# One block of a perceiver: every second query feature unit takes its minimum on GpSimd and its relu on VectorE instead of ScalarE

## The reference

```
x = x + cross_attention(layernorm(x), ctx)       # 16 heads, softmax over 512 context rows
x = x + linear_attention(layernorm(x))           # below
x = x + experts(layernorm(x))                    # 16 experts, top 8 tokens each, and a shared MLP of 1024

# linear attention, 16 heads of 32, 128 features
elu1(y) = where(y > 0, y + 1, exp(y))
q_proj = elu1(q @ proj);  k_proj = elu1(k @ proj)
kv  = sum over tokens of k_proj (x) v ;  k_sum = sum over tokens of k_proj
out = (q_proj @ kv) / (q_proj @ k_sum + 1e-8) @ w_out + b_out
```

## Time and profile before

| | |
|---|---|
| median of 3 executions | 666.02 us (664.43 to 666.73) |
| the profiled execution | 663.74 us, span 661.9 us |
| PE, DVE, ACT, POOL busy over the span | 96%, 47%, 39%, 5% |
| feature units of queries: exp, relu on ACT | 0.60, 0.59 us each, 16 of each |
| their joining instruction on DVE | 0.69 us each, 16 |
| granted TensorE clock | full in all stretches |

### The profile page before, as it was taken

One profiled execution on the slowest core, in us unless ns is written; L12 is line 12 of the kernel. 1 busy time (PEld: TensorE's weight loads), 2 busy tenths in 40 slices (PEclk: granted clock), 3 DMA queues, 4 the chain that ended last, 5 costly groups with the idle time before them and its releaser, 6 DMA issues.

```text
span 661.9 us, 10401 instructions
## 1 busy us (share of the span) xinstructions
PE 636.7 (96%) x4216; PEld 413.3 (62%) x4216; DVE 312.5 (47%) x643; ACT 255.4 (39%) x488; POOL 34.8 (5%) x38
## 2 busy tenths in 40 slices
PE   6989999999999999999998998999999999999997
PEld 5758777777778787678887664444444444343433
DVE  4965636354454516655778785423223222323123
ACT  5645536354545535546776252111121212211110
POOL 0300000000000000636000000000000000000000
PEclk9999999999999999999999999999999999999999
DMA  8211010101150000030319644989999999999972
GB/s 297 101 63 65 2 64 1 65 11 54 71 249 0 2 1 1 2 112 0 132 36 429 248 179 179 374 357 399 394 417 414 406 400 402 393 377 388 375 295 72
DMA packets 14347, 129.55 MB, mean 196 GB/s; under 512 B 2720, under 2 KB 2848, under 8 KB 6240
## 3 DMA queue, kind: packets, MB, share of 16 engines
q1 hardware_dynamic: 12576, 127.15, 49.1%
q10 hardware_dynamic: 1728, 1.77, 0.8%
HBM read 125.90 MB, written 1.05 MB: 192 GB/s over the span
## 4 chain that ended last, share of the span: by engine, by line
PE 78%; DVE 8%; DMA 5%; ACT 5%; ACTq 2%; issue 2%; SPq 1%; DVEq 0%
PE ps L1214 23%; PE ps L1501 14%; PE ps L1538 7%; PE ps L1511 5%; PE ps L1408 5%; DMA w_u<-in_wu 4%; PE ps L1284 4%; PE ps L1357 3%; PE ps L1551 3%; PE ps L1260 3%; PE ps L1295 2%; PE ps L1325 2%; PE ps L1455 2%; ACTq L396 2%; PE ps L1467 1%
## 5 line engine op out<-in xcount | busy, mean ns | idle before, releaser
L1538 PE MATMUL ps<-w_d,hid_T 128*64 128x512 f32 x256 | 58.2, 596 | 1.0 <-issue 0.7
L1501 PE MATMUL ps<-w_u,x_slot 128*64 128x512 f32 x256 | 58.1, 595 | 1.0 <-DMA w_u<-in_wu 1.0
L1501 PE MATMUL ps<-w_g,x_slot 128*64 128x512 f32 x256 | 58.1, 595 | 0.8 <-ACT x_slot L779 0.8
L582 ACT ACTIVATE probs<-ps,neg_max 128x512 f32<-128x512 f32 x64 | 43.5, 687 | 39.1 <-DVE neg_max L898 39.1
L741 ACT ACTIVATE hid<-ps 128x512 f32<-128x512 f32 x24 | 14.4, 598 | 102.6 <-PE ps L1501 76.8
L1214 PE MATMUL ps<-wv_hi,ctx_hi 128*128 128x512 f32 x128 | 51.6, 403 | 0.5 <-ACT v_s L563 0.5
L878 DVE COPY probs_T<-ps 128x512 f32<-128x512 f32 x28 | 19.4, 692 | 64.8 <-PE ps L1284 64.8
L1214 PE MATMUL ps<-wv_lo,ctx_hi 128*128 128x512 f32 x128 | 49.9, 390 | 0.0
L1214 PE MATMUL ps<-wv_hi,ctx_lo 128*128 128x512 f32 x128 | 49.9, 390 | 0.0
L898 DVE TENSOR_REDUCE neg_max<-ps 128x1 f32<-128x512 f32 x64 | 39.7, 682 | 18.4 <-PE ps L1260 18.3
L1076 DVE TENSOR_TENSOR hid<-hid,ps 128x512 f32<-128x512 f32 x24 | 16.5, 687 | 65.2 <-PE ps L1501 35.6
(11 more groups left out here) (246 smaller groups left out, 1183.0 us busy)
## 6 DMA issues: line engine op xcount, KB each, us to landing
w_u<-in_wu SPq DMA_DIRECT2D x16, 2048.0 KB, 15.7
w_d<-in_wd SPq DMA_DIRECT2D x16, 2048.0 KB, 12.0
w_g<-in_wg SPq DMA_DIRECT2D x16, 2048.0 KB, 13.2
ctx_raw<-in_ctx SPq DMA_DIRECT2D x7, 1024.0 KB, 4.8
w_qkv<-in_wqkv SPq DMA_DIRECT2D x1, 3072.0 KB, 15.2
ws_g<-in_wsg SPq DMA_DIRECT2D x1, 2048.0 KB, 7.8
ws_u<-in_wsu SPq DMA_DIRECT2D x1, 2048.0 KB, 7.9
ws_d<-in_wsd SPq DMA_DIRECT2D x1, 2048.0 KB, 21.3
```

The lines of the kernel that those rows point to most:

```text
L582: act.activation(probs[:, p, :], bank(SCORE[p]), ACT.Exp, bias=neg_max[:, p:p + 1], scale=1.0, accum_out=row_sum[:, p:p + 1]).then_inc(exp ...
L1501: ins = pe.matmul(ps[64 * fh:64 * (fh + 1), dst, :], x_slot[:, e, dt, :], weights[e % 2][:, dt, BANK * fh:BANK * (fh + 1)], start=(dt == 0 ...
L1538: ins = pe.matmul(ps[64 * fh:64 * (fh + 1), 6 + side(n), :], hid_T[:, side(n), j, 64 * fh:64 * (fh + 1)], w_d[e % 2][:, KT * fh + j, :], s ...
```

## The change

For odd units from 16 on (17, 19, ... 31: eight units) ACT does the exponential only. GpSimd takes the minimum with one, in place in `exps`, when `fexp_done` says that the exponential is there, and signals `fmin_done`. DVE waits for that and computes max(PSUM, 0) + exps in one instruction, which reads one operand from PSUM and one from SBUF. The even query units and all key units stay as they are. In GpSimd's stream the eight minima stand between the row bias and the wait for the output projection.

```diff
+        fmin_done = sem("fmin_done")
...
         def act_relus(u):
 
-            return u % 2 == 0 or u >= NT * KT
+            return u % 2 == 0
+
+        def pool_mins(u):
+
+            return not act_relus(u) and u >= NT * KT
...
             add_row_bias(1, bout_rows)
+            for u in range(2 * NT * KT):
+                if pool_mins(u):
+                    pool.wait_ge(fexp_done, u + 1)
+                    pool.tensor_scalar(exps[:, u % 3, :], exps[:, u % 3, :], 1.0, None, ALU.min).then_inc(fmin_done, 1)
             pool.wait_ge(res_ps, 2 * NT)
...
                                                  op1=ALU.add).then_inc(feat_done, 1)
+                    elif pool_mins(u):
+                        dve.wait_ge(fmin_done, sum(pool_mins(v) for v in range(u + 1)))
+                        dve.scalar_tensor_tensor(out=dst, in0=bank(u % 3), scalar=0.0, in1=exps[:, u % 3, :],
+                                                 op0=ALU.max, op1=ALU.add).then_inc(feat_done, 1)
```

## The result

The changed kernel took 669.98 us (median of 10 runs, 667.81 to 674.69) beside 664.75 us for the kernel before (10 runs on the same chip): a ratio of 1.0081, with an interval of 1.0062 to 1.0101. It is slower by 5.2 us, which is outside the 0.3% within which nothing could be told. One of the ten executions of before took 813.78 us, the other nine 663.21 to 666.73; without it their median is 664.43 and the loss 5.5 us, and the ratio compares undisturbed executions only. "The same" had been the likeliest, at 667.4 us; the median lies 0.02 us inside the upper end of the range. The profiled execution took 670.76 us, its span 668.7; that of before took 663.74 and 661.9.

A forecast was written before the change was run, and what follows sets the result against it. The prediction took TensorE, busy 96%, as the bound, with query units short through turn-taking waits. Delays of +0.6 at att(0,0), +1.0 by unit 27 and +1.3 by unit 31 became +1.4 on 666.02: 667.4 us, range 665.0 to 670.0.

The forecast's parts named there:

- "The same": Whole kernel: a time within about 0.3%, 2.0 us either way, of the kernel before; chance 0.61.
- What bounds the kernel: TensorE, busy 96% of the span; the change acts from 338.8 to 361.4 us, where TensorE idles 2.8 us.
- the number to watch: Start of att(1,0) on TensorE, 361.36 us before; forecast at 362.7 to 362.8.
- The break-even: Odd query units, exp to join: the new way takes 0.71 us plus the minimum, so it pays only under 0.49.
- the sum: Query units 17 to 31, step by step for a 0.70 us minimum: att(1,0) +1.4 us with collision, +0.4 without.
- The price of the minimum: GpSimd's minimum over 512 columns on an odd query unit: taken as 0.70 us, from 0.53 below to 1.29 above.
- the second rival: Slow GpSimd minimum, 1.17 to 1.29 us: end +4.2 us with collision, +2.3 without, 670.2 at the most; chance 0.19.
- its point of decision: Minimum of about 0.8 us, from where the loss with collision passes 2 us.
- The select plus slope estimate: GpSimd's minimum: select's 0.29 us for 128 columns plus 384 more at the memsets' 0.83 ns gives 0.61 us.
- The collision: VectorE's even joins and GpSimd's minima wait for each other at SBUF: +0.40 us a pair instead of +0.21.
- "Behind it nothing takes this up, so it keeps the 1.4": Behind att(1,0) TensorE is busy through 361.4 to 385 us, so the end moves by the same 1.4 us.
- The time between att(1,0) and the end: Sign from att(1,0) to the kernel's end: stays 300.5 us within one, else the forecast is wrong.

The follow-up runs named there:

- e5: Changed kernel with a plain GpSimd copy in place of the minimum (odd query units' minimum left out): 666.36 us, ratio 1.0018 to the kernel before.
- e1: Changed kernel with the eight minima on VectorE and none on GpSimd: 667.31 us, ratio 1.0034 to the kernel before.
- e6: Changed kernel with a GpSimd multiplication by 1.0 in place of the minimum: 670.61 us, ratio 1.0087 to the kernel before.
- e7: Changed kernel with even query units also joined from PSUM and exps, so no join has two SBUF operands: 670.35 us, ratio 1.0066.
- e2: Changed kernel with GpSimd's minimum over only 256 of the 512 columns: 667.62 us, ratio 1.004 to the kernel before.
- e10: Kernel before with the minima of only units 21 and 23 on VectorE, without their ScalarE relus: 663.99 us, ratio 0.998.
- e12: Changed kernel with only unit 25's minimum on GpSimd, other odd query units as in the kernel before: 666.21 us, ratio 1.0007.
- e4: Kernel before with VectorE's join of unit 31 run four more times, so TensorE waits longer, nothing on GpSimd: 671.16 us, ratio 1.0101.
- e8: Changed kernel with unused matmuls: two behind each query unit from 20, five ahead of att(1,0), eight in the routing: 668.75 us, ratio 1.0053.
- e9: Kernel before with unused matmuls: one behind each of units 20 to 23, four ahead of att(1,0), five in the routing: 663.12 us, ratio 0.9962.
- e3: Changed kernel with six unused matmuls on TensorE ahead of att(1,0): 670.20 us, ratio 1.0078 to the kernel before.
- e11: Kernel before with the minima of units 21 and 23 on VectorE plus the unused matmuls of e9: 663.59 us, ratio 0.9976.

## Why the prediction was wrong

**What bounds the kernel: right.** The place was right, and so was the number to watch. The change acts in the query stretch, att(1,0) is what it moves, and ScalarE's 3.9 us are worth nothing, since ScalarE only waits longer in their stead.

**The break-even: not contradicted, not tested below.** A minimum under 0.49 us was the condition. The copy of e5, at 0.61, loses 1.1 us (the interval's lower end is just above nothing), which is near the sum's +1.4 for 0.70; a part of the 1.1 may be the clock, 0.9965 on average there against 0.9974. No run had a GpSimd instruction under 0.49 us, so that one would pay is not shown; VectorE's minima of 0.42 in e1 did not.

**The price of the minimum: wrong, the step that failed first.** The prediction took 0.70 from the select and the memsets' slope, with 1.29 as the upper bound, since a tensor_tensor "reads two tiles". It was 1.49. The select plus slope estimate, 0.61, is by luck what a copy takes (e5), a form that wasn't in the change. The two-operand form wasn't an upper bound for the one-operand form with a scalar. Fed with 1.49, the steps of the second rival, which gave +2.3 without and +4.2 with the collision for 1.29, would say about +3 and +5; the profile has +3.53, near the steps without it. That rival had the right side and place, with a chance of 0.19, and its point of decision, 0.8 us, lies between e5 and e6 in time as in price. That the median still falls inside the range, by 0.02 us, is luck: the forecast of no change to be seen failed, and the range ended at 670.0 only because this rival, at 670.2 by its own steps, was cut off there. Nor do the chances follow from their terms: as written, these give about 0.03 or less for faster, 0.65 or more for the same and 0.32 for slower, not 0.05, 0.61 and 0.34.

By the Trainium skill, GPSIMD Engine Reference, section 4.1, GpSimd's operations with one input run at "roughly line-rate" and those with two some 2 times slower than VectorE's. The copy, 0.61 us for 512 columns, is not far from VectorE's 0.42 for the minimum; the tensor_scalar, 1.49, is 3.5 times that, and is slower than the two-input tensor_tensor at 1.29.

**The collision: there, but oversized.** A minimum that wants to start beside an even join is longer, and it is gone in e7. Yet it was worth 0.3 us, not the 1.0 (1.4 less 0.4) of the sum. In the profile after, the lengthenings on the chain add up to 0.70 us (0.50, 0.08 and 0.12), of which e7 gave back 0.32. With the minimum so long, it is the odd join that comes late; of the eight even joins three lengthen a minimum, one is held for 0.12 us, and four run in a gap of GpSimd's or well inside a minimum, where nothing is held.

By the Trainium skill, SBUF — State Buffer, section "SBUF: two separate sides", whoever starts first keeps the ports for its whole instruction. Where the join is first, the trace comes near to that: the minimum at 344.68 was 0.50 us longer, 1.99 in place of 1.49, beside a join of 0.68 us that had started 0.03 before it. The other way round it differs: the join at 356.99 lost 0.12 us where 1.14 us of the minimum were still to come. It was let go 0.47 us after the minimum had started. In e5 the same 0.47 us held beside a copy, of 0.61 us in all:

```profile
357.34 0.61 POOL L524 COPY exps<-exps 128x512 f32<-128x512 f32 x1 [1.99 <-ACT exps L698]
357.55 0.95 DVE L1018 SCALAR_TENSOR_TENSOR q_feat<-exps,relus 128x512 f32<-128x512 f32 x1
```

In e2, with 256 columns, it was 0.26 us (minimum at 359.95, join at 359.97 of 0.93 us instead of 0.69). So here the time for which GpSimd held the join went with its columns and not with the length of its instruction.

**"Behind it nothing takes this up, so it keeps the 1.4": wrong, the step that failed second.** The sum held every duration on TensorE fixed. But the more idle time the stretch has, the more often TensorE runs the work behind it at 1.2 GHz (mean clock 0.9941 instead of 0.9977): att(1,0) 5.41 us instead of 3.78 and, in the same profile, the routing's product 5.17 instead of 3.74, which e10 and e12 show behind a fast query stretch too. The time between att(1,0) and the end, which was to be 300.5 within one, grew by some 3. That idle TensorE is the cause is shown from both sides over many executions: added to the kernel before, it brings the low clock without GpSimd (e4, +5.9 us for a delay of 2.9); filled, the low clock is gone, with GpSimd's eight minima in place (e8) and in the kernel before (e9).

**Left open.** Why the routing's product at 406 us runs at the low clock in one execution and not in another isn't settled: the 21.50 us ahead of it have 2.97 us of idle TensorE after and 2.96 before, and ran at full clock in both. It took 5.0 us or more in the profiles of after, e2, e3, e5, e7, e10 and e12, and 3.7 in those of before, e1, e4 and e6, so a slow query stretch doesn't always bring it and isn't needed for it; with the fillers ahead of it (e8, e9, e11) it was 3.7 as well. The 1.43 us that it adds to the profile of after may thus be no effect of the change. Nothing here says what decides it from one execution to the next. Nor is the 5.2 us of the medians split exactly between the minimum and the clock. The best split is by runs at full clock: e8 took 668.75 us, the kernel before in its executions at full clock 663.75, and of the 5.0 between them 1.5 is the delay by fillers. The 3.5 left is the profile's 3.53 for the stage. The remaining 1.7 of the 5.2 (2.0 of the 5.5 without the execution of 813.78) is then the clock's, net of what it had cost the kernel before already; the mean clocks had given 2.4.

## What to carry to other kernels

Price an operation on GpSimd by a row of its own form, tensor_scalar by a tensor_scalar; a row with more operands is no upper bound, and a missing row is worth a wide range. Where a change gives TensorE more waiting, count what the same matmuls cost at half clock behind it, and look at the mean granted clock of every run of the kernel before: here 0.997 or less in 53 of 79 meant that 2.2 us could be had. A few matmuls without use, put where TensorE waits anyway, were worth 0.4% here, more than any of the shifts of work between the other engines that were run.

## What the runs showed of the hardware that was not expected

- GpSimd's tensor_scalar on 128 partitions of float32 costs 2.5 ns a column and 0.2 us besides (0.845 us for 256 columns, 1.49 for 512), minimum and product alike; its copy of the same tile 0.61 us, and VectorE's minimum 0.42.
- TensorE was granted 1.2 GHz for 3.5 to 7 us behind stretches in which none of its waits was long: 5.8 us idle out of 26.1, the longest wait 1.64 us (kernel after), and in e1 behind 3.5 us idle out of 22.55, where the kernel before has 2.8 out of 22.6 and kept 2.4 GHz in its profile.
- With one gap filled the mean clock stayed at 0.994 (e3); with all of them filled it was 0.999 or more in every execution (e8, e9).
- An even join that starts 0.35 us into a minimum is held for only 0.12 us, and one that starts 0.55 us or more into it isn't held at all, though the minimum runs for another 0.9 us. The hold ended 0.47 us after the start of a minimum or copy of 512 columns, 0.26 us after that of a minimum of 256.
